# Quantised FFN weights packed as bf16 rows in their load buffers and turned by transposing transfers, in place of turns on TensorE

## The reference, cut to what matters

```
h = layernorm(x)
q, k, v    = h @ wq.T + bq,  h @ wk.T + bk,  h @ wv.T + bv
q2, k2, v2 = q @ wiq.T + biq, k @ wik.T + bik, v @ wiv.T + biv      # 16 heads of 64
scores = einsum('hnd,hmd->hnm', q2, k2) / 8 + mask                  # mask scattered from 6528 edges
x = x + (softmax(scores) @ v2) @ wo.T + bo

h = layernorm(x);  xq = act_fake_quant(h, clip_x)
gate = xq @ weight_fake_quant(w_gate).T          # w_gate, w_up: (352, 1024)
up   = xq @ weight_fake_quant(w_up).T
h2   = act_fake_quant(silu(gate) * up, clip_down)
x = x + h2 @ weight_fake_quant(w_down).T         # w_down: (1024, 352)
```

## Time and profile before

| | |
|---|---|
| median of 3 runs | 336.85 us (335.77 to 340.67) |
| the profiled execution | 334.56 us, of which the span from the first to the last instruction is 332.7 us |
| TensorE matmuls, busy | 322.2 us, 97% of the span |
| VectorE | 225.6 us, 68% |
| ScalarE | 182.3 us, 55% |
| GpSimd | 187.0 us, 56% |
| moved by transfers | 41.71 MB, at a mean of 125 GB/s |

### The profile page before, as it was taken

How to read it: one execution, slowest core, us unless ns; L and a number is a source line. 1 busy time by engine, 2 the same in 40 slices (tenths; PEclk the granted TensorE clock), 3 DMA queues, 4 the chain that set the end, 5 groups by cost and what they waited for, 6 DMA issues and landing times.

```text
span 332.7 us, 5989 instructions
## 1 busy us (share of the span) xinstructions
PE 322.2 (97%) x2086; PEld 297.1 (89%) x2086; DVE 225.6 (68%) x600; ACT 182.3 (55%) x333; POOL 187.0 (56%) x253
## 2 busy tenths in 40 slices
PE   4999999999999999999999999999999999999994
PEld 4899998878999999999999999999999877887864
DVE  3857898856255556554185977879797875497574
ACT  4847257464333333333375968668595865243562
POOL 5686668547777766789816484563726757000000
PEclk9999999999999999999999999999999999999999
DMA  7997335667234333493411240302213110000005
GB/s 257 367 406 283 126 129 167 215 195 236 65 122 129 128 122 126 127 338 113 141 65 66 68 149 36 128 21 108 70 57 128 64 66 0 0 2 0 2 0 191
DMA packets 16763, 41.71 MB, mean 125 GB/s; under 512 B 3440, under 2 KB 7392, under 8 KB 16736
## 3 DMA queue, kind: packets, MB, share of 16 engines
q1 hardware_dynamic: 13824, 38.87, 34.1%
q0 software_dynamic: 2064, 1.80, 1.8%
q10 hardware_dynamic: 848, 0.70, 0.6%
HBM read 37.99 MB, written 3.37 MB: 124 GB/s over the span
## 4 chain that ended last, share of the span: by engine, by line
PE 90%; DVE 4%; DMA 2%; ACT 1%; POOL 1%; issue 1%; SPq 0%; DVEq 0%; ACTq 0%
PE PS L756 65%; PE PS L913 5%; PE PS L901 5%; PE PS L889 4%; PE PS L1048 2%; PE PS L737 1%; DMA V<-in_w_down 1%; DMA X<-in_x 1%; PE PS L1102 1%; PE PS L825 1%; PE PS L815 1%; PE PS L747 1%; PE PS L800 1%; PE PS L819 1%; POOL QT L460 1%; PE PS L790 1%
## 5 line engine op out<-in xcount | busy, mean ns | idle before, releaser
L422 POOL TENSOR_TENSOR ring<-stage,ring 128x256 fp32r<-128x256 f32 x124 | 90.3, 765 | 39.3 <-ACT ring L507 36.7
L756 PE MATMUL PS<-XT,ring 128*128 128x384 f32 x528 | 93.3, 335 | 0.0
L756 PEld LDWEIGHTS PS<-XT,ring 128*128 128x128 f32 x528 | 91.4, 188 | 0.1
L440 POOL DMA_INDIRECT codes<-ecol,place x51 | 60.3, 1182 | 26.4 <-issue 14.2
L507 ACT ACTIVATE ring<-stage 128x1024 fp32r<-128x1024 f32 x52 | 54.3, 1057 | 6.2 <-DMA stage<-in_weights 2.3
L614 ACT ACTIVATE scratch<-scratch,smx 128x384 f32<-128x384 f32 x48 | 28.9, 604 | 18.5 <-DVE smx L1345 18.5
L756 PE MATMUL PS<-QT,ring 128*128 128x384 f32 x192 | 35.5, 338 | 0.0
L756 PE MATMUL PS<-AT,ring 128*128 128x384 f32 x192 | 35.2, 338 | 0.0
L756 PEld LDWEIGHTS PS<-AT,ring 128*128 128x128 f32 x192 | 33.0, 188 | 1.5 <-issue 1.5
L756 PE MATMUL PS<-ring,AT 128*128 128x512 f32 x144 | 34.1, 393 | 0.0
L1249 DVE TENSOR_TENSOR ring<-stage,ring 128x1024 fp32r<-128x1024 f32 x21 | 25.7, 1227 | 12.1 <-issue 8.4
(11 more groups left out here) (200 smaller groups left out, 466.5 us busy)
## 6 DMA issues: line engine op xcount, KB each, us to landing
stage<-in_weights SPq DMA_DIRECT2D x56, 512.0 KB
V<-in_w_gate_up SPq DMA_DIRECT2D x4, 512.0 KB, 7.6
codes<-scratch SPq DMA_DIRECT2D x3, 576.0 KB, 14.5
X<-in_x SPq DMA_DIRECT2D x3, 512.0 KB, 5.2
out<-X SPq DMA_DIRECT2D x4, 384.0 KB, 2.6
scratch<-codes POOLq DMA_DIRECT2D x2, 576.0 KB, 5.7
scratch<-in_w_gate_up SPq DMA_DIRECT2D x2, 512.0 KB
V<-in_w_down SPq DMA_DIRECT2D x5, 176.0 KB, 5.2
```

The lines of the kernel that those rows point to most:

```text
L422: ins = pool.tensor_tensor(ring[1][:, slot, piece], stage[:, slot % STAGE, piece], ring[0][:, slot, piece].bitcast(F32), ALU.subtract)
L440: pool.indirect_dma_start(codes[b].rearrange("(n a) -> n a", a=1), bass.IndirectOffsetOnAxis(ap=place[:, t:t + 1], axis=0), ecol[:, VAL, t ...
L756: ins = pe.matmul(outs, lhs[a], rhs[b], start=start and n == 0, stop=stop and n == 2, skip_group_check=True)
```

## The change

In each `ffn_take`, ScalarE packs the down tile and then the gate or up tile as bf16 rows into the same buffer that holds them (`dn_rows`, `gu_rows`), waits until both are written (`rows_packed`), and issues from its own queue two transposing transfers, which write `wdT` and `guT` (one for steps 3 and 7, whose `s % 4` is 3). There are eight for the down tiles, of three blocks of 128 columns, and six for gate and up, of eight. `ffn_turn`, `gu_ps`, the 24 down turns and the three `down_take` are gone, and `wdN` is replaced by `wdT`. A refill waits on the landing of the transfers of the buffer's last step (`rows_turned`, one semaphore a step, `BUF_FREE`), and so do ScalarE before it writes the inner V into `V2`, and GpSimd before it loads the tables into `scratch`. TensorE waits for all eight before the gate and up matmuls. Where the down turns stood, eight `keep_clock` matmuls stand.

```diff
         guT = sb("guT", [P, KT, 2 * I_F], BF16)
-        wdN = sb("wdN", [P, KT, I_F], BF16)
+        wdT = sb("wdT", [P, IT, C], BF16)
         ident = sb("ident", [P, P], F32)
...
-        gu_ps = PS[:, 2, :].bitcast(F16).rearrange("p (k i) -> p k i", k=KT)
-        DN_BANK = (6, 2, 0)
-        wdT = stage[:, 2:4, :].rearrange("p s c -> p (s c)").bitcast(BF16)[:, 0:IT * C].rearrange("p (i c) -> p i c", i=IT)
-        def dn_ps(i):
-            return PS[:, DN_BANK[i], :].bitcast(BF16)
...
+        gu_rows = [a[:, 0, :].bitcast(BF16) for a in gu_in]
+        dn_rows = [a.bitcast(BF16)[:, 0:IT * P] for a in dn_in]
+        ROWS_PACKED = (2, 4, 6, 7, 9, 11, 13, 14)
+        BUF_FREE = {3: 0, 4: 1, 5: 2, 6: 4, 7: 5}
...
         ffn_q = sem("ffn_q")
-        ffn_full = sem("ffn_full")
-        ffn_evac = sem("ffn_evac")
-        down_packed = sem("down_packed")
-        down_full = sem("down_full")
-        down_ready = sem("down_ready")
+        rows_turned = [sem(f"rows_turned{s}") for s in range(KT)]
+        rows_packed = sem("rows_packed")
         up_seen = sem("up_seen")
...
-            def load_ffn(s, taken):
-                if taken:
-                    sp.wait_ge(ffn_evac, taken)
+            def load_ffn(s):
+                if s in BUF_FREE:
+                    sp.wait_ge(rows_turned[BUF_FREE[s]], 32)
                 i, j = s // 4, s % 4
...
             sp.wait_ge(t_full, KT)
-            load_ffn(0, 0)
-            load_ffn(1, 0)
+            load_ffn(0)
+            load_ffn(1)
             next_chunk(4)
-            load_ffn(2, 0)
+            load_ffn(2)
             next_chunk(5)
...
                 next_chunk(c)
-            load_ffn(3, 1)
+            load_ffn(3)
             next_chunk(13)
-            load_ffn(4, 2)
-            load_ffn(5, 3)
+            load_ffn(4)
+            load_ffn(5)
             next_chunk(14)
             next_chunk(15)
-            load_ffn(6, 4)
+            load_ffn(6)
             next_chunk(16)
-            load_ffn(7, 5)
+            load_ffn(7)
             for c in range(17, 20):
...
             pool.wait_ge(bo_added, 2 * NT)
-            pool.wait_ge(ffn_full, 6)
-            pool.wait_ge(down_packed, 8)
+            pool.wait_ge(rows_turned[5], 32)
+            pool.wait_ge(rows_turned[7], 16)
             for b in range(LISTS):
...
-                i, j = s // 4, s % 4
+                i, j, buf = s // 4, s % 4, FFN_BUF[s]
                 act.wait_ge(ffn_q, s + 1)
-                act.activation(wdN[:, s, :], dn_half[FFN_BUF[s]], ACT.Identity, bias=minus[:, 0:1]).then_inc(down_packed, 1)
+                act.activation(dn_rows[buf][:, 0:I_F], dn_half[buf], ACT.Identity, bias=minus[:, 0:1]
+                               ).then_inc(rows_packed, 1)
                 if j < IT:
                     i0, iw = I_TILES[j]
-                    act.wait_ge(ffn_full, IT * i + j + 1)
-                    act.activation(guT[:, :, I_F * i + i0:I_F * i + i0 + iw], gu_ps[:, :, 0:iw], ACT.Identity,
-                                   bias=minus[:, 0:1]).then_inc(ffn_evac, 1)
+                    act.activation(gu_rows[buf][0:iw, :].rearrange("p (b c) -> p b c", b=2), gu_half[buf][0:iw, :, :],
+                                   ACT.Identity, bias=minus[0:iw, 0:1]).then_inc(rows_packed, 1)
+                act.wait_ge(rows_packed, ROWS_PACKED[s])
+                act.dma_start_transpose(wdT[:, :, s * P:(s + 1) * P], dn_rows[buf]).then_inc(rows_turned[s], 16)
+                if j < IT:
+                    act.dma_start_transpose(guT[:, :, I_F * i + i0:I_F * i + i0 + iw], gu_rows[buf][0:iw, :]
+                                            ).then_inc(rows_turned[s], 16)
...
                 if s % 4 == 3:
-                    act.wait_ge(ffn_full, (4, 6)[s // 4])
-                    act.wait_ge(down_packed, (5, 8)[s // 4])
+                    act.wait_ge(rows_turned[(3, 6)[s // 4]], (16, 32)[s // 4])
                     for m in range(NT):
...
-            def down_take(i):
-                iw = I_TILES[i][1]
-                act.wait_ge(down_full, i + 1)
-                act.activation(wdT[0:iw, i, :], dn_ps(i)[0:iw, :], ACT.Copy).then_inc(down_ready, 1)
-            down_take(0)
-            down_take(1)
             act.wait_ge(h_scale, 1)
...
                                scale=gmx[0:iw, 12:13]).then_inc(ht_ready, 1)
-            down_take(2)
             act.wait_ge(dsc_ready, 1)
...
-            def ffn_turn(s):
-                if s % 4 == IT:
-                    return
-                n = IT * (s // 4) + s % 4
-                pe.wait_ge(ffn_q, s + 1)
-                if n:
-                    pe.wait_ge(ffn_evac, n)
-                buf, iw = FFN_BUF[s], I_TILES[s % 4][1]
-                for k in range(KT):
-                    ins = pe.transpose(gu_ps[:, k, 0:iw], gu_half[buf][0:iw, k // 4, k % 4 * P:(k % 4 + 1) * P],
-                                       turner[0:iw, 0:iw])
-                ins.then_inc(ffn_full, 1)
...
                         keys(g)
-                if s > 5:
-                    ffn_turn(s - 6)
...
                 finish(ins)
-                if c < 6:
-                    ffn_turn(c + 2)
...
             low_half, high_half = range(4), range(4, KT)
+            for s in range(KT):
+                pe.wait_ge(rows_turned[s], 32 if s % 4 < IT else 16)
             for part in range(2):
...
                         gate_up(g, i, high_half).then_inc(gu_full, 1)
-            for i, (i0, iw) in enumerate(I_TILES):
-                if i == 1:
-                    pe.wait_ge(sig_ready, 1)
-                if i == 2:
-                    pe.wait_ge(up_seen, 1)
-                for s in range(KT):
-                    ins = pe.transpose(dn_ps(i)[0:iw, s * P:(s + 1) * P], wdN[:, s, i0:i0 + iw], wide[:, 2 * P:3 * P])
-                ins.then_inc(down_full, 1)
+            keep_clock(8, red_columns, 6)
             spread_max(1, 8, NT + 1)
...
                     if j == 0:
-                        pe.wait_ge(down_ready, max(i + 1, 2))
                         pe.wait_ge(hq_ready, i + 1)
```

## The result

The kernel with the change takes 344.83 us (median of 4 runs, 344.18 to 348.77), the kernel before 336.91 (4 runs, 335.77 to 340.67) on the same chip: a ratio of 1.0289, 95% interval 1.023 to 1.0349. It is slower. The profiled execution took 344.36 us, with a span of 342.6 (332.7 before); so 9.9 us are to be found.

The account below looks back on a forecast made before the run. TensorE, 90% of the chain, was taken as the bound. Chunk 14 5.6 us later (turns' 2.75 us gain included) plus 1.4 for the clock, 7.0 us, lifts the profiled 334.56 to 341.6; 2.3 more for the median gives 344, range 336.5 to 355.

Parts of the forecast that it names:

- Gone from TensorE: Front part: six turns of eight matmuls leave TensorE, with one 0.31 us idle; 2.75 us, the most the edit can give.
- T: Time a pair of transfer issues holds ScalarE behind a pack; taken as 2.9 us, between 0.66 and 4.06.
- L: Time from the second issue of a pair to the landing; taken as 2.3 us, upper end 5.2.
- The chain: Buffer 0's steps 1, 4 and 6: refills wait for issues and landings, so TensorE starts chunk 14 5.6 us later.
- The clock: TensorE's clock falls in the 5.4 us wait before chunk 14; 1.4 us lost, between 0 and 4.2.
- Traffic: Loads slowed by the turning transfers beside them; priced at nothing.
- The tail: At the end, eight clock-keeping matmuls replace 24 down turns that lie beside VectorE's work; nothing on both sides.
- As cheap as plain ones: Rival: T near 0.7 to 1.3 and L near 2.3 give 0 to +1.5 us, 337 to 338; chance 0.20.
- Faster: Rival: T + L under 2.9, no low part late, TensorE keeps all 2.75 us of the turns, 334; chance 0.05.
- Issues that block: Rival: a pair holds ScalarE for 6 us, so ScalarE itself is the chain; +17 us, 354; chance 0.15.

Follow-up runs that it names:

- e13: e8 measured once more (gate and up by turning transfers from areas of their own, down tiles as before); 344.83 us, ratio 1.0223 to the kernel before.
- e11: e8 with its six gate and up transfers made plain copies without turning; 335.35 us, ratio 0.996 to the kernel before.
- e4: The kernel with the change plus 24 filling matmuls on TensorE ahead of chunk 14; 344.26 us, ratio 1.0289 to the kernel before.
- e9: The kernel with the change, VectorE doing only chunk 14's low part ahead of step 6; 351.6 us, ratio 1.0384 to the kernel before.
- e6: The kernel before with only gate and up turned by transfers, down tiles packed into `wdN` as before; 343.85 us, ratio 1.0151.
- e7: The kernel with the change, but gate and up turned on TensorE again, only down tiles by transfers; 343.58 us, ratio 1.0168 to the kernel before.
- e10: The kernel with the change, its fourteen transfers made plain copies without turning; 342.74 us, ratio 1.0194 to the kernel before.
- e5: The kernel with the change, its transfers issued from SyncE's load queue instead of ScalarE's; 343.24 us, ratio 1.0265 to the kernel before.
- e2: The kernel with the change, rows packed into separate areas so refills from step 4 wait for packing, not landing; 342.67 us, ratio 1.0219 to the kernel before.
- e8: The kernel before with gate and up by turning transfers from three areas of their own, no refill waiting for a landing; 342.47 us, ratio 1.01.
- e1: The kernel with the change, VectorE doing low parts of chunks 12 to 15 ahead of FFN steps; 348.47 us, ratio 1.0406 to the kernel before.

## Why the prediction was right, and where it wasn't

The direction, the place and the time (344.0, measured 344.83) came out, the time partly by luck, because errors cancel. By the start of the Q stage 6.7 us were gone, where 7.0 were forecast in all. But the profiled execution was forecast at 341.6 and took 344.36: 3.2 us came in the K stage, from no term of the sum, and they stand in for the 2.3 us that the prediction added between the profiled execution and the median.

**Gone from TensorE: right.** 2.75 us of turns were the gain to be had; the Q stages of e13 and e11, which hardly waited, began 2.4 and 2.8 us early.

**T: right for the pair, wrong in its parts.** 2.9 us was taken from GpSimd's indirect issues, as 0.97 for three blocks and 1.93 for eight; measured were 1.20 and 1.36, 2.6 in all. The time hardly grows with the number of blocks, so the sum came out near by luck. The estimate from the Trainium skill's table (DMA: Bandwidth & Descriptors, Why a DMA increments its semaphore by 16 and not by 1) was 2.6 for the pair.

**L: right in the chain, wrong behind it.** Predicted 2.3; measured 2.2 and 1.9 before the two refills that count. But the landing of step 6's transfer took 5.6 us here, 9.9 in e4 and 13.6 in e9. The step that failed is "ScalarE's copies of the inner V wait for transfers that landed before TensorE is done with them". These copies set when the Q stage could begin.

**The chain: right, 1.4 us too long.** With the measured terms: step 0's lateness T - 1.91 = 0.7, step 1's T + L = 4.8, step 4's T + L - 2.36 = 2.1, and the two loads +0.3 and -0.6, are 7.3; less TensorE's 3.45 us of slack, 3.9. Chunk 14 began 4.9 us late, of which 0.67 stood already at 42.76 us, ahead of every transfer, so 4.2. The waits of 2.22, 0.65 and 4.08 us stand for the predicted 2.2, 1 and 5.4, the refills at 60.87 and 75.26 for 60.7 and 75. e6, e7 and e10 bear the mechanism out, with the reservation that T, which the formula counts three times, is not worth that much: e10 halved it and got the refills out only 0.8 us earlier, since the transfers landed 4.0 and 2.6 us after their issues for 2.2 and 1.9, and e5 took it from ScalarE for nothing.

**The clock: right in size, wrong as a term.** 1.4 us were predicted and 1.4 are there. But the Q stage could not begin before the copies at 93.03, so they lie beside a wait: without them the stage would have begun at 93.68 all the same, and e4, which kept chunk 14 at full clock, is no faster. Where no landing hides it, it counts: in e10 the copies didn't wait for a transfer, chunks 14 and 15 took 10.88 us, 2.5 more than 8.35, and the Q stage began that much later.

**Traffic: priced at nothing, which holds for the two refills of this kernel and not elsewhere.** Step 4's load ran beside step 2's transfers, issued at 61.36 and 62.59, and took 5.0 us; step 6's ran beside step 5's, issued at 77.53 and 78.75, and took 4.1; before, both took 4.7. The price shows where transfer and refill are issued together: 5.6 to 9.1 us in e2, e8 and e13. By the Trainium skill (DMA: Bandwidth & Descriptors, Issuing engines are not separate DMA queues) transfers share the same DMA engines whichever engine starts them; e2, e8 and e13 agree, where ScalarE's transfers slowed loads of SyncE's queue.

**The tail: right**, nothing.

**Not foreseen: 3.2 us in the K stage.** ScalarE stood still from 129.00 to 135.26, TensorE waited 0.99 and 1.58 us behind it, and 69.82 us lie between the stages where 66.58 did. The unchanged kernel's profile and those of e1, e2, e4, e5 and e9 have no such pause, those of e6 to e8 and e10 to e13 have one or more. On the chip of e1, e2, e4 and e5 the kernel before stayed within 334.59 to 335.64 us, on the others it went up to over 340 us. So I take the pause for something outside the program and not for an effect of the change; that is argued, not shown, and the kernel with the change itself was not measured on that even chip, which would have told. Until then about a third of the 9.9 us is without a cause. e2, without it, still loses 2.2%.

**Rivals.** "As cheap as plain ones" (337 to 338) fails by the issue, and e10, where the issue was as cheap as that, is at 1.0194 and not at the 1.005 that this case gives: a landing ahead of each refill is enough. "Faster" needed T + L under 2.9, and it was 4.8 and 4.5. "Issues that block" fails by T.

## What to carry to other kernels

When a buffer's refill waits for the landing of a transfer that reads it, each such turn of the buffer costs an issue and a landing (3.4 to 4.8 us here where ScalarE issues it, 4.5 and 4.8 for 352 KB, 3.4 and 3.9 for 96 KB), in place of an engine's 1.1 us copy; count how many lie in a row ahead of the engine that sets the end. Turning on an engine at 97% looks dear and cost 0.44 us a tile; the transfer that replaced it was slower than all the slack around it. And look for every wait on such a landing, also those "far behind": the last one here, on a landing of 5.6 us, hid what the clock cost, and in e4 and e9 a landing of 9.9 and 13.6 us took back what the repair had won.

## What the runs showed that I hadn't expected

- The turning transfer's issue mostly holds ScalarE for 1.20 us (128x384) and 1.25 to 1.39 us (128x1024; single ones took up to 2.5): eight blocks against three, and hardly more time. Plain copies of the same tiles take 0.60 and 0.66. It takes as long on the load queue of SyncE (1.2 and 1.3).
- The turning transfers that a refill waited for landed 1.8 to 3.5 us after the end of their issue in the kernel with the change, 1.3 to 5.7 us over all runs. Step 6's, with weight chunks being loaded beside it, took 5.6, 9.9 and 13.6 us in three kernels that issue it at nearly the same time (87.44, 86.37, 86.72); why so differently stays open.
- Halving the issue (e10) didn't bring the loads behind it forward.
